# The last phase of a two-layer graph network moved into the second layer's block: sums by GpSimd and TensorE, rows normalised by ScalarE, stored chunk by chunk

## The chip, the core and the metric

One Trainium2 chip, one core. The metric is the device time of the kernel in microseconds, the median of three runs. All times inside the kernel are counted from the start of the span of one profiled execution.

## The reference

Two message-passing layers over a graph of 3125 nodes (160 features: 64 scalars and 32 vectors of 3) and 100,000 edges; each is added to its input and followed by a layer norm. The second one is what matters here:

```python
agg = segment_sum(tp, src, num_segments=N) / DENOM      # tp: one message for each edge
out_s = agg_s @ W_out_s + skip_s                        # 96 wide
out_v = einsum('nmi,mk->nki', agg_v, W_out_v) + skip_v  # 32 vectors of 3
fs = silu(out_s[:, :64])
gv = sigmoid(out_s[:, 64:96])[:, :, None] * out_v
x = layernorm(x + concatenate([fs, gv.reshape(N, -1)]))
```

`silu(a)` is `a * sigmoid(a)`, so one sigmoid of 96 columns gives both gates.

## The kernel before

Nodes are padded to 3200 rows, that is 25 tiles of 128 (`NT`), taken in 5 chunks (`NC`) of 5 tiles (`FT`). Edges are taken in 392 pairs of tiles (`NPAIR`). The first layer runs from 0 to about 1100 us, a node phase follows (`nodes`), and from about 1260 us the second layer (`second_layer`) goes through the pairs: messages are projected by TensorE, summed over equal sources, and added into one of four tables in device memory by GpSimd's indirect DMAs (`scatter`, L681). A table row has 192 columns (`OW`): 96 scalars and 3 x 32 vector columns. Pair `u` with even `u` goes into tables 0 and 1, with odd `u` into tables 2 and 3, so the last four of these DMAs go into tables 0, 1, 2, 3 in this order. After the last, GpSimd waits for all four tables (L688), and the block ends: every engine meets the others there.

The last phase is a block of its own (`c5`, L1257 to L1354):

- SyncE issues ten loads of tables 0 and 1, ScalarE ten of tables 2 and 3 (480 KB each, chunk by chunk, L1275 and L1293). `tabs` has room for all five chunks.
- `sums(m)` on VectorE adds tables 0 and 1 of chunk `m` (L1315), GpSimd adds tables 2 and 3 (L1286), VectorE adds the two halves into `so` (L1318).
- ScalarE takes the sigmoid of 96 columns for each of the chunk's 5 tiles (L1297).
- `update(m - 1)` on VectorE multiplies (L1324, L1325), adds to `xres` (L1330), and takes mean and variance of the 5 tiles (L1333, L1336).
- When all chunks are through, ScalarE takes the roots of all 25 variances (L1299), VectorE refines them (L1362 to L1366) and normalises tile by tile, two instructions for each (L1348, L1350), which also puts the vector columns into the order of the output. SyncE stores a chunk when its five tiles are done (L1278).

On each engine instructions run in the order in which they are written, and DMAs are issued from the engine's own order too.

Of the kernel before, what the change touches and what calls it, by code (L numbers as in the profile page):

```python
# [29 lines left out]
FT = 5  # L30
P = 128
# [31 lines left out]
NPAIR = TILES // 2  # L63
EPS = 1e-5
# [16 lines left out]
def steps(eng, total, body, first, unroll):  # L81

    first = min(-(-first // unroll) * unroll, total)
    last = max(first, total // unroll * unroll)
    for s in range(first):
        body(s, s // unroll, s % unroll)
    if last > first:
        with eng.Fori(first // unroll, last // unroll) as j:
            for r in range(unroll):  # L90
                body(j * unroll + r, j, r)
    for s in range(last, total):
        body(s, s // unroll, s % unroll)

# [11 lines left out]
def gnn_kernel(nc, t, out):  # L106
    top = ExitStack()
    with top:
# [286 lines left out]
        with ExitStack() as cs:  # L395
# [101 lines left out]
            goht_done, gx_ready, gstep, gfeat_done = (sem(cs, n) for n in ("goht_done", "gx_ready", "gstep", "gfeat_done"))  # L497
            joined = sem(cs, "joined")
            block = cs.enter_context(nc.Block())

# [114 lines left out]

            @block.gpsimd
            def _(pool):
# [69 lines left out]
                for tab in range(NTAB):  # L687
                    pool.wait_ge(tab_in[tab], 16 * (TILES // NTAB))  # L688

            @block.scalar  # L690
            def _(act):
# [102 lines left out]
                split_steps(act, NPAIR, 2, step, 4, short=2)  # L794

# [12 lines left out]
            def _(pe):  # L808
# [446 lines left out]
        c4.close()  # L1255

        with ExitStack() as c5:  # L1257
            tabs = sb(c5, "tabs", [P, NC, NTAB, FT, OW])
            tsum = sb(c5, "tsum", [P, 2, 2, FT, OW])
            so = sb(c5, "so", [P, 2, FT, OW])  # L1260
            sg = sb(c5, "sg", [P, 2, FT, 96])
            upd = sb(c5, "upd", [P, 2, FT, D])
            bst5 = sb(c5, "bst5", [P, NT, 6])
            orow = sb(c5, "orow", [P, NC, FT, D])
            tin = [sem(c5, f"tin{i}") for i in range(NC)]
            half_done, half2_done, so_done, sg_done, upd_done, res_done, bs5, mv5 = (
                sem(c5, n) for n in ("half_done", "half2_done", "so_done", "sg_done", "upd_done", "res_done", "bs5", "mv5"))
            lv5, lr5, on_done, ch5, o_out = sem(c5, "lv5"), sem(c5, "lr5"), sem(c5, "on_done"), sem(c5, "ch5"), sem(c5, "o_out")
            block = c5.enter_context(nc.Block())

            @block.sync
            def _(sp):
                for m in range(NC):
                    for k in range(2):
                        sp.dma_start(tabs[:, m, k, :, :], tile_rows(t["tabs"][k], m)).then_inc(tin[m], 16)  # L1275
                for m in range(NC):
                    sp.wait_ge(on_done, m + 1)
                    sp.dma_start(tile_rows(out, m), orow[:, m, :, :]).then_inc(o_out, 16)  # L1278
                sp.wait_ge(o_out, 16 * NC)

            @block.gpsimd
            def _(pool):
                for m in range(NC):
                    pool.wait_ge(tin[m], 16 * NTAB)
                    since(pool, so_done, m - 1)
                    pool.tensor_tensor(tsum[:, m % 2, 1, :, :], tabs[:, m, 2, :, :], tabs[:, m, 3, :, :],  # L1286
                                       ALU.add).then_inc(half2_done, 1)

            @block.scalar
            def _(act):  # L1290
                for m in range(NC):
                    for k in range(2, NTAB):
                        act.dma_start(tabs[:, m, k, :, :], tile_rows(t["tabs"][k], m)).then_inc(tin[m], 16)  # L1293
                for m in range(NC):
                    act.wait_ge(so_done, m + 1)
                    since(act, upd_done, m - 1)
                    act.activation(sg[:, m % 2, :, :], so[:, m % 2, :, 0:96], ACT.Sigmoid).then_inc(sg_done, 1)  # L1297
                act.wait_ge(lv5, 1)
                act.activation(ntmp[:, 0, :], ntmp[:, 1, :], ACT.Sqrt).then_inc(lr5, 1)  # L1299

            @block.vector
            def _(dve):
                done = [0]

                def link(ins):

                    done[0] += 1
                    ins.then_inc(ch5, 1)
                    dve.wait_ge(ch5, done[0])

                def sums(m):

                    r = m % 2
                    dve.wait_ge(tin[m], 16 * NTAB)
                    dve.tensor_tensor(tsum[:, r, 0, :, :], tabs[:, m, 0, :, :], tabs[:, m, 1, :, :], ALU.add).then_inc(half_done, 1)  # L1315
                    dve.wait_ge(half_done, m + 1)
                    dve.wait_ge(half2_done, m + 1)
                    dve.tensor_tensor(so[:, r, :, :], tsum[:, r, 0, :, :], tsum[:, r, 1, :, :], ALU.add).then_inc(so_done, 1)  # L1318

                def update(m):  # L1320

                    r = m % 2
                    dve.wait_ge(sg_done, m + 1)
                    dve.tensor_tensor(upd[:, r, :, 0:S], so[:, r, :, 0:S], sg[:, r, :, 0:S], ALU.mult)  # L1324
                    dve.tensor_tensor(upd[:, r, :, S:D].rearrange("p a (c u) -> p a c u", c=3),  # L1325
                                      so[:, r, :, 96:OW].rearrange("p a (c u) -> p a c u", c=3),
                                      sg[:, r, :, S:96].unsqueeze(2).to_broadcast([P, FT, 3, V]), ALU.mult).then_inc(upd_done, 1)
                    dve.wait_ge(upd_done, m + 1)
                    here = xres[:, m * FT:(m + 1) * FT, :]
                    dve.tensor_tensor(here, here, upd[:, r, :, :], ALU.add).then_inc(res_done, 1)  # L1330
                    dve.wait_ge(res_done, m + 1)
                    for u in range(m * FT, (m + 1) * FT):
                        dve.bn_stats(bst5[:, u, :], xres[:, u, :]).then_inc(bs5, 1)  # L1333
                    for u in range(m * FT, (m + 1) * FT):
                        dve.wait_ge(bs5, u + 1)
                        dve.bn_aggr(mv[:, u, :], bst5[:, u, :]).then_inc(mv5, 1)  # L1336

                for m in range(NC + 1):
                    if m < NC:
                        sums(m)  # L1340
                    if m:
                        update(m - 1)
                dve.wait_ge(mv5, NT)
                layer_norm_scale(dve, link, mv, ntmp, rstd, lv5, lr5, slice(0, NT), 1)
                for u in range(NT):
                    m, at = divmod(u, FT)
                    mean, scale = mv[:, u, 0:1], rstd[:, u:u + 1]
                    dve.tensor_scalar(orow[:, m, at, 0:S], xres[:, u, 0:S], mean, scale, ALU.subtract, ALU.mult)  # L1348

                    last = dve.tensor_scalar(orow[:, m, at, S:D].rearrange("p (u c) -> p c u", c=3),  # L1350
                                             xres[:, u, S:D].rearrange("p (c u) -> p c u", c=3), mean, scale,
                                             ALU.subtract, ALU.mult)
                    if at == FT - 1:
                        last.then_inc(on_done, 1)  # L1354
# [83 lines left out]
```

## Time and profile before

| | |
|---|---|
| median of 3 runs | 2825.72 us (2823.81 to 2827.75) |
| profiled execution | 2825.36 us, its span 2823.5 us, 1.86 us around it |
| last indirect DMA issued by GpSimd | 2748.66 us |
| first load of a table issued | 2755.02 us |
| last VectorE instruction ends | 2820.34 us |
| TensorE's mean granted clock | 0.92 of full speed |

The profiled execution is 0.36 us below the median of the three runs, so differences inside its span can be set against the median.

### The profile page before, as it was taken

To read this page: it belongs to the slowest core of one execution; us is meant where nothing else is said; L and a number is where in the kernel's file an instruction comes from. 1 tells how busy PE (TensorE), PEld (TensorE's weight loads), DVE (VectorE), ACT (ScalarE), POOL (GpSimd) and SP (SyncE) were. 2 spreads that over 40 slices of the span, in tenths; PEclk is the share of its full clock that TensorE was granted. 3 is DMA by queue.
4 is the path that set the end of the run, shared out by engine and by line. 5 is a ranking of instruction groups with operands and counts; after the bars stand their busy time and mean duration, and the time that the engine had idled before them with its cause. 6 is when DMAs were issued, how large, how long until landed. Compare 5 with 4: busy or idle time off the path is not lost. (4 is left out here: it accounts for less than half of the span.)

```text
span 2823.5 us, 80757 instructions
## 1 busy us (share of the span) xinstructions
PE 2604.4 (92%) x24172; PEld 2231.0 (79%) x24172; DVE 1632.9 (58%) x4318; ACT 887.5 (31%) x1988; POOL 2071.6 (73%) x1825
## 2 busy tenths in 40 slices
PE   4799999999999998979999999999999999999970
PEld 2477777777777777868999999999999999999960
DVE  5365555555555555515666666666666666666646
ACT  1111111111111112124444444444444444444430
POOL 3477777777777775236888888888888888888881
PEclk9999899898889888559999999999999999999985
DMA  4333333333333333247888878888888888878765
GB/s 129 106 110 102 107 100 105 101 106 101 101 103 106 102 101 81 99 159 134 143 143 143 142 143 143 143 143 143 143 143 144 143 144 141 145 142 144 141 98 168
DMA packets 388993, 355.58 MB, mean 126 GB/s; under 512 B 60992, under 2 KB 340928, under 8 KB 388416
## 3 DMA queue, kind: packets, MB, share of 16 engines
q0 software_dynamic: 150528, 141.40, 33.4%
q1 hardware_dynamic: 228256, 204.77, 25.7%
q10 hardware_dynamic: 10176, 9.03, 1.1%
q8 instruction: 14, 0.23, 0.0%
q14 instruction: 19, 0.16, 0.0%
HBM read 244.75 MB, written 135.90 MB: 135 GB/s over the span
## 5 line engine op out<-in xcount | busy, mean ns | idle before, releaser
L681 POOL DMA_INDIRECT tab<-summed,sidx x784 | 1218.0, 1554 | 272.2 <-issue 208.9
L634 POOL DMA_INDIRECT gat<-f,gidx x784 | 764.8, 976 | 247.8 <-issue 228.6
L1147 DVE TENSOR_TENSOR prod<-ps_w,xg 128x768 f32<-128x768 f32 x392 | 375.3, 958 | 281.5 <-issue 169.7
L937 PE MATMUL ps_o<-ro_v,prod 128*128 128x96 f32 x3136 | 478.2, 275 | 0.0
L937 PEld LDWEIGHTS ps_o<-ro_v,prod 128*128 128x128 f32 x3136 | 413.2, 192 | 0.0
L927 PE MATMUL ps_w<-hid,wf 64*128 64x128 f32 x4704 | 368.7, 289 | 1.2 <-DVE prod L1147 1.2
L773 ACT ACTIVATE xg<-ps_x 128x768 f32<-128x768 f32 x392 | 296.3, 808 | 199.5 <-PE ps_x L959 193.9
L927 PEld LDWEIGHTS ps_w<-hid,wf 64*128 64x128 f32 x4704 | 293.5, 187 | 69.4 <-issue 44.6
L946 PE MATMUL ps_d<-msg,same 128*128 128x193 f32 x1568 | 332.4, 334 | 1.3 <-ACT summed L792 1.3
L935 PE MATMUL ps_o<-ro_s,prod 96*128 96x96 f32 x1568 | 329.9, 292 | 0.6 <-DVE msg L1158 0.6
L1016 DVE TENSOR_TENSOR ta<-ps_w,gat 128x512 f32<-128x512 f32 x196 | 135.5, 691 | 295.4 <-DMA gat<-f,gidx 237.4
L801 PEld LDWEIGHTS ps_g<-sel,ta 128*128 128x128 f32 x1568 | 208.4, 207 | 116.3 <-issue 59.6
L801 PE MATMUL ps_g<-sel,ta 128*128 128x96 f32 x1568 | 242.2, 302 | 42.3 <-DVE acc_c L1028 40.7
L935 PEld LDWEIGHTS ps_o<-ro_s,prod 96*128 96x128 f32 x1568 | 235.5, 189 | 48.3 <-issue 0.9
L786 ACT ACTIVATE msg<-ps_o 128x192 f32<-128x192 f32 x392 | 130.3, 332 | 445.8 <-PE ps_o L937 444.0
L702 ACT ACTIVATE h<-ps_h 128x256 f32<-128x256 f32 x196 | 75.3, 384 | 593.8 <-PE ps_h L820 583.9
L1154 DVE TENSOR_TENSOR ash<-ps_o,sh 128x192 f32<-128x192 f32 x392 | 140.1, 357 | 191.6 <-ACT msg L786 183.2
L946 PEld LDWEIGHTS ps_d<-msg,same 128*128 128x128 f32 x1568 | 247.9, 192 | 1.6 <-DVE msg L1158 1.6
L792 ACT ACTIVATE summed<-ps_d 128x386 f32<-128x386 f32 x392 | 193.1, 493 | 162.8 <-PE ps_d L946 156.8
L827 PE MATMUL ps_w<-w,h 64*128 64x192 f32 x1568 | 205.2, 384 | 0.0
L827 PEld LDWEIGHTS ps_w<-w,h 64*128 64x128 f32 x1568 | 141.6, 209 | 75.6 <-issue 75.5
L801 PE MATMUL ps_g<-sel,tc 128*96 128x72 f32 x1568 | 193.3, 272 | 0.0
(183 smaller groups left out, 3354.8 us busy)
## 6 DMA issues: line engine op xcount, KB each, us to landing
src_bc<-in_src_rows SPq DMA_DIRECT2D x196, 256.0 KB
tabw<-feat SPq DMA_DIRECT2D x784, 36.0 KB
ea<-in_ea SPq DMA_DIRECT2D x196, 128.0 KB
feat<-fst SPq DMA_DIRECT2D x25, 576.0 KB, 2.8
gat<-f,gidx POOLq DMA_INDIRECT x784
hot_dst<-in_dst_rows SPq DMA_DIRECT2D x98, 128.0 KB
hot_dir<-sh_rows SPq DMA_DIRECT2D x98, 128.0 KB
dst_bc<-hot_dst SPq DMA_DIRECT2D x196, 64.0 KB
```

Of the source, the lines that this page charges most:

```text
L634: pool.indirect_dma_start(out=gat[:, r % 4, k, :], out_offset=None, in_=t["f0"], in_offset=bass.IndirectOffsetOnAxis(ap=gidx[:, r // 4, at ...
L681: pool.indirect_dma_start(out=t["tabs"][into[k]], out_offset=bass.IndirectOffsetOnAxis(ap=sidx[:, r, k:k + 1], axis=0), in_=summed[:, r, k ...
L773: act.activation(xg[:, r, 2 * i:2 * i + 2, :], ps_x4[:, 2 * i:2 * i + 2, 0:3 * P], ACT.Copy)
L792: act.activation(summed[:, ur, :, :], ps_d[:, :, 0:LW], ACT.Copy).then_inc(sum_done, 1)
L801: last = pe.matmul(ps_g[r][0:hi, (n * 4 + lo) * WIN:(n * 4 + up) * WIN], lhs[:, r, k, :, :].rearrange("p a b -> p (a b)"), sel[:, r, k, lo ...
L827: last = pe.matmul(ps_w[r][:, k, 0:192], h2[h:h + S, r, P * (k % 2):P * (k % 2) + P], w3[h:h + S, :], start=True, stop=True)
L927: last = pe.matmul(ps_w4[:, h, P * c:P * c + P], wf2[rows_h, c, :], hid[rows_h, r // 2, at], start=True, stop=True)
L935: pe.matmul(ps_o[:, k, 0:96], prod[0:96, ur % 2, k, 0, :], ro_s[0:96, :], start=True, stop=True)
L937: last = pe.matmul(ps_o[:, k, 96 + 64 * c:192 + 64 * c], prod[:, ur % 2, k, 1 + c, :], ro_v[:, c, :], start=True, stop=True)
L946: last = pe.matmul(ps_d[:, k, 0:LW], same[:, ur // 2, ur % 2 * 2 + k, :], msg[:, ur % 2, k, :], start=True, stop=True)
L1147: dve.tensor_tensor(prod[:, r % 2, :, :, :].rearrange("p k c e -> p k (c e)"), ps_w4[:, :, 0:3 * P], xg[:, r // 2, r % 2 * 2:r % 2 * 2 + 2 ...
L1154: dve.tensor_tensor(ash[:, :, :, :], ps_o[:, :, 96:128].unsqueeze(2).to_broadcast([P, 2, 3, V]), sh[:, bass.ds(u * 2, 2), :].unsqueeze(3). ...
```

## The change

The block `c5` is gone. Its work is appended, on each engine, to the instructions of the second layer in the block before it.

- **Loads.** `load_tables` runs on SyncE for tables 0 and 1 and on ScalarE for 2 and 3. Ahead of the first load of table `k` it waits for that table's scatters alone. `tabs` has room for four chunks (`RING5`), so the fifth chunk's loads wait for the sum of chunk 0 (`so_ready`, `pair_done`).
- **Sums.** GpSimd adds tables 0 and 1 (`pair`). TensorE adds table 2, table 3 and that sum by multiplying each with the identity and accumulating in PSUM: 3 matmuls of 480 columns for each of two halves, f32. Ahead of it, after the last edge pair, TensorE does 10 matmuls of 512 columns whose result nobody reads (`idle_matmuls`).
- **Gate and update.** ScalarE's sigmoid and VectorE's products read the sum from PSUM. The residual is added in two parts, the second of which already writes the output's order of columns, into `orow`, which takes the place of `f1`.
- **Roots.** Each chunk by itself: GpSimd raises the five variances to the power -0.5 (`root5`), VectorE refines in four instructions and makes `-mean * scale` (`scale5`).
- **Normalising.** ScalarE, one activation for each tile: `Identity(scale * x + shift)`, both operands a column (`normalise`). SyncE stores the chunk after its five.

The orders on the engines, for chunks 0 to 4 (g is the gate, n normalise, u update, s scale, p pair, r root):

```
ScalarE  g0 g1 n0 g2 n1 g3 n2 g4 n3 n4
VectorE  u0 u1 s0 u2 s1 u3 s2 u4 s3 s4
GpSimd   p0 p1 r0 p2 r1 p3 r2 p4 r3 r4
```

```diff
+def idle_matmuls(pe, bank, square, count, times=4):
+    for _ in range(count):
+        pe.matmul(bank, square, square.unsqueeze(1).to_broadcast([P, times, P]), start=True, stop=True)
...
+            def load_tables(eng, tables, landed):
+                for m in range(NC):
+                    since(eng, so_ready, m + 1 - RING5)
+                    since(eng, pair_done, m + 1 - RING5)
+                    for k in tables:
+                        if m == 0:
+                            eng.wait_ge(tab_in[k], 16 * (TILES // NTAB))
+                        eng.dma_start(tabs[:, m % RING5, k, :, :], tile_rows(t["tabs"][k], m)).then_inc(landed[m], 16)
...
+                load_tables(sp, (0, 1), tin_a)
+                for m in range(NC):
+                    sp.wait_ge(on_done, FT * (m + 1))
+                    sp.dma_start(tile_rows(out, m), orow[:, m * FT:(m + 1) * FT, :]).then_inc(o_out, 16)
...
-                for tab in range(NTAB):
-                    pool.wait_ge(tab_in[tab], 16 * (TILES // NTAB))
+                def pair(m):
+                    pool.wait_ge(tin_a[m], 32)
+                    since(pool, so_ready, m - 1)
+                    pool.tensor_tensor(tsum[:, m % 2, :, :], tabs[:, m % RING5, 0, :, :], tabs[:, m % RING5, 1, :, :],
+                                       ALU.add).then_inc(pair_done, 1)
+                def root5(m):
+                    tiles = slice(m * FT, (m + 1) * FT)
+                    pool.wait_ge(lv5, m + 1)
+                    pool.tensor_tensor(ntmp[:, 0, tiles], ntmp[:, 1, tiles], a2_col[:, tiles], ALU.pow).then_inc(lr5, 1)
...
+                for m in range(NC + 1):
+                    if m < NC:
+                        pair(m)
+                    if m:
+                        root5(m - 1)
...
+                def gate(m):
+                    act.wait_ge(so_ready, m + 1)
+                    since(act, upd_done, m - 1)
+                    act.activation(sg[:, m % 2, :, :], ps_so[m % 2][:, 0, :, :], ACT.Sigmoid).then_inc(sg_done, 1)
+                def normalise(m):
+                    act.wait_ge(shift_done, m + 1)
+                    for u in range(m * FT, (m + 1) * FT):
+                        act.activation(orow[:, u, :], orow[:, u, :], ACT.Identity, scale=rstd[:, u:u + 1],
+                                       bias=shift[:, u:u + 1]).then_inc(on_done, 1)
+                load_tables(act, (2, 3), tin_b)
+                for m in range(NC + 1):
+                    if m < NC:
+                        gate(m)
+                    if m:
+                        normalise(m - 1)
...
+                pe.wait_ge(relu_done, NGRP)
+                idle_matmuls(pe, ps_x4[:, 0, :], ident[:, :], 10)
+                for m in range(NC):
+                    pe.wait_ge(tin_b[m], 32)
+                    since(pe, sg_done, m - 1)
+                    since(pe, upd_done, m - 1)
+                    pe.wait_ge(pair_done, m + 1)
+                    for h in range(2):
+                        for n, part in enumerate((tabs[:, m % RING5, 2, :, :], tabs[:, m % RING5, 3, :, :], tsum[:, m % 2, :, :])):
+                            last = pe.matmul(ps_so[m % 2][:, h, :, :], ident[:, :], part[:, :, 96 * h:96 * h + 96],
+                                             start=n == 0, stop=n == 2)
+                    last.then_inc(so_ready, 1)
...
+                    dve.tensor_tensor(orow[:, chunk, 0:S], xres[:, chunk, 0:S], upd[:, r, :, 0:S], ALU.add)
+                    dve.tensor_tensor(orow[:, chunk, S:D].rearrange("p a (u c) -> p a c u", c=3),
+                                      xres[:, chunk, S:D].rearrange("p a (c u) -> p a c u", c=3),
+                                      upd[:, r, :, S:D].rearrange("p a (c u) -> p a c u", c=3), ALU.add).then_inc(res_done, 1)
...
+                def scale5(m):
+                    dve.wait_ge(lr5, m + 1)
+                    link5(dve.tensor_tensor(tmp, first, first, ALU.mult))
+                    link5(dve.tensor_tensor(tmp, tmp, var, ALU.mult))
+                    link5(dve.tensor_scalar(tmp, tmp, -0.5, 1.5, ALU.mult, ALU.add))
+                    link5(dve.tensor_tensor(scale, first, tmp, ALU.mult))
+                    dve.scalar_tensor_tensor(tmp, mv[:, chunk, 0], -1.0, scale, ALU.mult, ALU.mult).then_inc(shift_done, 1)
+                for m in range(NC + 1):
+                    if m < NC:
+                        update5(m)
+                    if m:
+                        scale5(m - 1)
```

## Rows read from the trace of the kernel before

**Rows 1.** The chain that ended last, in time: start us, us, what.
```profile
2773.79 2.91 ACTq L1293
2776.72 1.28 ACT L1297
2778.65 0.64 DVE upd L1324
...
2820.03 0.31 DVE orow L1350
```

**Rows 2.** Timeline, end of the scatters: start us, us, engine, line, idle before.
```profile
2744.97 1.54 POOL L681 DMA_INDIRECT tab<-summed,sidx  x1 [0.30 <-DMA tab<-summed,sidx]
...
2748.66 1.54 POOL L681 DMA_INDIRECT tab<-summed,sidx  x1 [0.31 <-issue]
2755.02 20.17 SPq L1275 DMA_DIRECT2D tabs<-tab  x10
```

**Rows 3.** Busy time in stretches of 1 us; the last columns: clock, DMA share, GB/s.
```profile
2751.00:2752.00 1.00, 0.00 (x0) 0.00 (x0) 0.00 (x0) 0.00 (x0) 0.00 (x0) 0.50 0.62 83
2752.00:2753.00 1.00, 0.00 (x0) 0.00 (x0) 0.00 (x0) 0.00 (x0) 0.00 (x0) 0.50 0.00 0
...
2756.00:2757.00 1.00, 0.00 (x0) 0.00 (x0) 0.00 (x0) 0.00 (x0) 0.00 (x0) 0.50 0.66 93
...
2787.00:2788.00 1.00, 0.00 (x0) 0.00 (x0) 0.96 (x3) 0.25 (x1) 0.01 (x1) 0.50 0.09 27
```

**Rows 4.** Groups of instructions from 2762 us on: busy us, mean ns, idle before.
```profile
L1315 DVE TENSOR_TENSOR tsum<-tabs 128x960 f32<-128x960 f32 x5 | 6.1, 1224 | 27.1 <-DMA tabs<-tab 27.1
L1330 DVE TENSOR_TENSOR xres<-xres,upd 128x800 f32<-128x800 f32 x5 | 5.0, 991 | 0.2
L1325 DVE TENSOR_TENSOR upd<-so,sg 128x480 f32<-128x480 f32 x5 | 3.2, 648 | 0.0
L1297 ACT ACTIVATE sg<-so 128x480 f32<-128x480 f32 x5 | 2.9, 599 | 18.5 <-DVE so L1318 18.4
L1324 DVE TENSOR_TENSOR upd<-so,sg 128x320 f32<-128x320 f32 x5 | 2.5, 509 | 3.5 <-ACT sg L1297 3.5
```

**Rows 5.** Timeline: GpSimd's add alone, then GpSimd and VectorE together.
```profile
2776.74 2.21 POOL L1286 TENSOR_TENSOR tsum<-tabs 128x960 f32<-128x960 f32 x1 [2.85 <-DMA tabs<-tab]
...
2787.62 0.99 DVE L1330 TENSOR_TENSOR xres<-xres,upd 128x800 f32<-128x800 f32 x1
2787.99 2.69 POOL L1286 TENSOR_TENSOR tsum<-tabs 128x960 f32<-128x960 f32 x1 [2.39 <-DMA tabs<-tab]
2788.65 1.23 DVE L1333 BATCH_NORM_STATS2 bst<-xres 128x6 f32<-128x160 f32 x5
...
2790.14 1.56 DVE L1315 TENSOR_TENSOR tsum<-tabs 128x960 f32<-128x960 f32 x1
```

**Rows 6.** Groups elsewhere in the kernel, shapes kept apart.
```profile
L285 ACT ACTIVATE frow<-ps_n,a_col 128x160 f32<-128x160 f32 x25 | 9.8, 393 | 49.8 <-PE ps_n L261 49.8
L728 ACT ACTIVATE f<-ps_y 128x160 f32<-128x160 f32 x25 | 7.6, 305 | 44.4 <-PE ps_y L889 44.4
L665 POOL TENSOR_SCALAR fst<-f 128x32 f32<-128x32 f32 x75 | 22.2, 296 | 0.0
L1364 DVE TENSOR_TENSOR ntmp<-ntmp 128x5 f32<-128x5 f32 x5 | 0.9, 171 | 0.2
```

**Rows 7.** Timeline: TensorE's last matmuls of 193 columns.
```profile
2732.27 0.85 PE L946 MATMUL ps_d<-msg,same 128*128 128x193 f32 x4
```

**Rows 8.** Busy time in stretches (PE first), the third column from the end: granted clock.
```profile
1116.00:1120.00 4.00, 4.00 (x21) 4.00 (x21) 2.04 (x9) 3.89 (x6) 0.00 (x0) 0.50 0.60 205
...
1276.00:1280.00 4.00, 2.99 (x32) 2.77 (x36) 2.82 (x5) 0.47 (x2) 0.00 (x0) 0.97 0.55 142
...
2735.00:2737.00 2.00, 0.33 (x3) 0.04 (x1) 0.00 (x0) 0.00 (x0) 1.70 (x2) 1.00 0.50 56
2737.00:2740.00 3.00, 0.00 (x0) 0.00 (x0) 0.38 (x2) 0.49 (x1) 2.39 (x3) 0.53 0.50 46
```

More of the change, by code:

```diff
@@ L63 @@
 NPAIR = TILES // 2
+RING5 = 4
 EPS = 1e-5
@@ L686, in _ @@
                 steps(pool, NPAIR, scatter, 4, 4)
-                for tab in range(NTAB):
-                    pool.wait_ge(tab_in[tab], 16 * (TILES // NTAB))
+                def pair(m):
[7 more added lines that the diff above has]
+                    pool.tensor_tensor(ntmp[:, 0, tiles], ntmp[:, 1, tiles], a2_col[:, tiles], ALU.pow).then_inc(lr5, 1)
+                pool.memset(a2_col[:, :], -0.5).then_inc(half_set, 1)
+                pool.wait_ge(half_set, 1)
+                for m in range(NC + 1):
[3 more added lines that the diff above has]
+                        root5(m - 1)
             @block.scalar
@@ L1253, in _ @@
                     second_layer(sweep)
[L1255 to L1307, printed above, removed]
-                    ins.then_inc(ch5, 1)
[L1309 to L1322, printed above, removed]
@@ L1323, in update, with link5, update5 @@
+                done5 = [0]
+                def link5(ins):
+                    done5[0] += 1
+                    ins.then_inc(ch5, 1)
+                    dve.wait_ge(ch5, done5[0])
+                def update5(m):
+                    r, so = m % 2, ps_so[m % 2]
+                    chunk = slice(m * FT, (m + 1) * FT)
                     dve.wait_ge(sg_done, m + 1)
-                    dve.tensor_tensor(upd[:, r, :, 0:S], so[:, r, :, 0:S], sg[:, r, :, 0:S], ALU.mult)
+                    dve.tensor_tensor(upd[:, r, :, 0:S], so[:, 0, :, 0:S], sg[:, r, :, 0:S], ALU.mult)
@@ L1331, in update @@
                     dve.wait_ge(res_done, m + 1)
                     for u in range(m * FT, (m + 1) * FT):
-                        dve.bn_stats(bst5[:, u, :], xres[:, u, :]).then_inc(bs5, 1)
+                        dve.bn_stats(bst5[:, u, :], orow[:, u, :]).then_inc(bs5, 1)
                     for u in range(m * FT, (m + 1) * FT):
@@ L1336, in update @@
                         dve.bn_aggr(mv[:, u, :], bst5[:, u, :]).then_inc(mv5, 1)
+                    dve.wait_ge(mv5, (m + 1) * FT)
+                    dve.tensor_scalar(ntmp[:, 1, chunk], mv[:, chunk, 1], EPS, None, ALU.add).then_inc(lv5, 1)
+                def scale5(m):
+                    chunk = slice(m * FT, (m + 1) * FT)
+                    first, var, scale, tmp = ntmp[:, 0, chunk], ntmp[:, 1, chunk], rstd[:, chunk], shift[:, chunk]
+                    dve.wait_ge(lr5, m + 1)
[4 more added lines that the diff above has]
+                    dve.scalar_tensor_tensor(tmp, mv[:, chunk, 0], -1.0, scale, ALU.mult, ALU.mult).then_inc(shift_done, 1)
                 for m in range(NC + 1):
                     if m < NC:
-                        sums(m)
+                        update5(m)
                     if m:
[L1342 to L1354, printed above, removed]
+                        scale5(m - 1)
+        c4.close()
 def layer_norm_scale(dve, link, mv, ntmp, rstd, var_ready, root_ready, tiles, turn):
```

19 lines of the change are left out of this document (16 added, 3 removed).

## The prediction

> **What bounds the kernel now.** I read the chain that ended last first, since only what lies on it can be gained. Before the last phase the change alters nothing, so the question is what happens between the last scatter and the end. GpSimd issues the last scatter at 2748.66 [rows 2] and its data moves until about 2752.0 [rows 3]; the first loads are issued at 2755.02 [rows 2]. In the chain ScalarE's own loads come next: its tenth is issued from 2773.79 to 2776.7, since the queue takes no more than it can hold, and only then can ScalarE load its table (1.28 us) and do the first gate, which ends at 2778.63 [rows 1]. From 2778.65 to 2820.34 VectorE is the chain [rows 1]: 41.7 us, ending with the 50 normalising instructions. The store needs the remaining 3.16 us to the end of the span at 2823.5. The loads are no bound in that stretch: their data moves from about 2756.3 to 2787.1 [rows 3], 9.83 MB in 30.8 us, 320 GB/s, and VectorE is behind them.
>
> So the change can gain by an earlier first gate, and by a shorter way from there to the last store.
>
> **The first gate.** ScalarE waits for tables 2 and 3 only and not for the blocks to meet: its first load goes out at about 2750.4 and the second at 2752.3, 2.7 us ahead of 2755.02. SyncE's tables 0 and 1 are complete two DMAs earlier, 3.7 us [rows 2], so its loads run alone from about 2748 to 2752. ScalarE's ten stay its limit. Its tenth was issued when the flow had 10.4 us to go [rows 1, 3], that is 3.5 of its transfers at 2 x 0.49 MB / 320 GB/s = 3.07 us each. Now 6.5 of them must have moved since about 2751.5 (1.3 us from an issue to the first data, as 2755.0 to 2756.3 [rows 2, 3]): 6.5 x 3.07 = 20.0 gives 2771.5. I take 2771.0, as SyncE's lead and its fifth chunk's wait leave ScalarE's queue a bit more of the rate. Table load and gate [rows 1, 4]: 1.28 + 0.60 gives **2772.9**, 5.7 us earlier than 2778.63. Had the lead no effect at all, it would be 2775.
>
> **Costs for each chunk.**
>
> Update on VectorE: 0.40 and 0.65 for the two products (L1324's 509 ns less 0.1 that lies under the next one, and L1325's 648 [rows 4]); the addition of 320 elements 0.43 and of 480, with columns reordered, 0.65 + 0.15 + 0.03, where there was one of 0.99 [rows 4]; statistics 1.5 from their start to that of the next addition [rows 5], with 0.1 as that now has to wait for their end; one more small instruction 0.18 [rows 6]. Sum **4.1**. The 0.15 for reordering is an estimate between 0 and 0.4.
>
> Scale on VectorE: five small dependent instructions of 0.17 with 0.03 between [rows 6], **1.0**.
>
> Normalise on ScalarE: an activation of 160 elements took 305 ns without, 393 with one column operand [rows 6]; with two I estimate 480. They overlap by 0.1, so five take 5 x 0.38 + 0.1 = **2.0**.
>
> GpSimd's pair: 2.2 alone [rows 5]. Its power of 5 elements has no row. Bounds: nothing, and the 2.2 us of its widest add; I take 0.3, as the row nearest in size, 32 elements in 296 ns [rows 6]. This is the least certain price.
>
> TensorE's sum: two matmuls of 193 columns, two records each, last 0.85 us together [rows 7]; less some 0.15 of start-up, an estimate, that is 0.9 ns for a column and record. Six matmuls of 480 columns: 6 x 2 x 480 x 0.9 = **5.2 us** at the full clock, 10.3 at half. The ten idle matmuls (512 columns, 9.2 us) are over at about 2744.5. The clock was at 1.00 up to 2737 and at 0.53 over 2737 to 2740, when TensorE had stopped at 2735.3 [rows 8]. So I expect them to hold 2.4 GHz until some 2 to 4 us behind their end, and chunk 0's sum, which waits for table 3's data until about 2759, to start at 1.2 GHz. They cost nothing, being behind TensorE's last work, and bring nothing.
>
> **A lock between GpSimd and VectorE.** VectorE's add at 2790.14 took 1.56, against a mean of 1.22 with itself included [rows 4]: it ended 1.02 after GpSimd's add, which ended at 2790.68. And that one took 2.69 instead of 2.21 alone; it ended 2.07 after VectorE's addition, which ended at 2788.61 and overlapped it. The statistics in between took the same 1.23 [rows 5]. So two such adds exclude each other. The Trainium skill ("SBUF — State Buffer", section "SBUF: two separate sides") says the same of VectorE's instructions with two SBUF inputs against GpSimd's reads, an exclusive lock for the whole instruction. That VectorE's products, which read one input from PSUM now, are spared by it, no row shows; were they not, pair 2 would stall VectorE by 1 us more.
>
> **The new order makes waits.** p2 on GpSimd is written behind r0, which needs u0's variance; p3 behind r1, p4 behind r2. So each of these pairs starts just when VectorE has finished an update: p2 falls into u1 (its additions wait, 1.5 us), p3 into s0 and p4 into s1, whose small adds of two SBUF inputs wait 2.2 us each. On ScalarE g2 is behind n0, which needs s0, and u2 needs g2: between s and the next u VectorE stands idle for n + g, 2.0 + 0.6 + 0.05, three times (before u2, u3, u4).
>
> **The sum from the first gate's end.** 2772.9; five updates 20.5; p2's stall 1.5; five scales, less the overlaps of their ends, 4.6; power 4 x 0.3 = 1.2; p3 and p4 in the scales 4.4; n + g three times 8.0; at the end n3 and n4 behind the last scale 3.1. That gives 2816.2, where VectorE ended at 2820.3: the way from the first gate has become 43.3 us instead of 41.7, so 1.6 of the 5.7 us won are given back. The store takes 3.16 as before: **2819.4** for the span, 4.1 us less. VectorE's normalising and its ten adds of tables (1.2 us each by L1315 [rows 4]) are gone, but the waits for ScalarE and GpSimd stand in their place. TensorE hides: p2 ends at 2779.6, sum 2 by 2784.8 at the full clock, and g2 cannot start before 2787.9. With 1.86 us around the span and the 0.36 by which the profiled run lies under the median, the forecast is **2821.6**, 0.15% less.
>
> **Rivals.**
>
> *The clock stays at half.* The five sums then take 10.3 us each and are a chain: 2759 to 2769, 2779.6 (sum 1), then from p2 on 2790, 2800.2, 2810.5; g4 ends at 2811.2, u4, s4, n4 and the store follow: span 2823.8, time **2826.0**, no change. For it: at 1116 TensorE was busy the whole 4 us at 0.50 [rows 8], with weight loads all that time. Against: the clock rose at about 1276 [rows 8]. By the Trainium skill ("TensorE: Matmul & The Clock Gate", section "The HAM clock gate (the "warmup" mystery)") sustained matmuls release it, and the sums would not bind; that gives the forecast of 2821.6. Chance 0.2, the forecast 0.42.
>
> *The adds hardly collide.* If GpSimd's adds find no VectorE instruction in their way and the reverse (or the pairs get ahead), p2, p3 and p4 cost nothing: the span is 2813.4 at the full clock, 2816.0 if a sum takes 7.7 us; time 2815.6 to 2818.2, **2816.5**. Chance 0.22. Against it are rows 5.
>
> *The power is dear.* It lies ahead of s and, by r1 and r2, ahead of p3 and p4; 1 us more costs 4 to 5 us in all, once at each chunk. From 1.2 us on the kernel is slower than before; at 2.2, the upper bound, the span is 2827.0, time **2829**; from 2.6 us on, or at 2.2 with the clock at half, it is slower by over 0.2%. Nothing but the missing row speaks for it. Chance 0.12.
>
> *Table swaps.* Identity has no row; Copy and Relu needed no table of their own. If it did, gates and normalising would each load one: seven more of 1.28 us, six of them on the chain, 2829. 
>
> **Range and chances.** From the case without collisions, 2815.5, to the dear power, 2829; the forecast's own range is 2819 to 2824 (reordering 0 to 0.4 five times, first gate up to 2 us later). About 0.2% (5.6 us) is what a measurement can tell. Faster by more: the second rival and a third of the forecast's case, 0.37. Within: the rest of it, the half clock, the table swaps, a part of the dear power, 0.53. Slower: the rest of the dear power, beyond its bound or with the half clock, 0.10.
>
> **What would show it.** First loads at about 2747 (SyncE) and 2750.4 (ScalarE); the first gate ends near 2773; three idle stretches of 2.7 us on VectorE ahead of u2, u3, u4, ended by ScalarE's gate and not by TensorE; the pow's mean near 0.3 us; scales 0 and 1 with one instruction of over 2 us; TensorE's sum 5 to 8 us. If the gates wait for TensorE, the clock was it; if the chain shows GpSimd ahead of the scales, the power. I am wrong if ScalarE's loads no longer hold back the first gate, or if the last phase starts earlier than the scatters let me think.

## The result, and the profile after

The changed kernel takes **2809.31 us** (median of 7 runs, 2805.9 to 2815.2) where the kernel before, beside it, takes 2827.33 (7 runs, 2823.81 to 2832.56): ratio **0.9944**, 95% interval 0.9931 to 0.9958. Forecast were 2821.6 us and a range of 2815.5 to 2829. It is faster by more than the forecast allowed, and the first question is where.

The profiled execution took 2810.92 us, its span 2809.1. The end of the scatters and the new loads, from the timeline (start, duration, engine, line, operation; idle time before it in brackets):

```profile
2738.11 25.98 SPq L529 DMA_DIRECT2D tabs<-tab  x10
...
2740.11 1.55 POOL L717 DMA_INDIRECT tab<-summed,sidx  x1 [0.30 <-issue]
...
2744.24 19.97 ACTq L529 DMA_DIRECT2D tabs<-tab  x10
...
2764.24 1.28 ACT L852 ACT_TABLE_LOAD   x1 [34.73 <-issue]
...
2765.53 0.57 ACT L852 ACTIVATE sg<-ps_x 128x480 f32<-128x480 f32 x1
```

The last scatter, L717, is issued at 2740.11; before it was 2748.66 [rows 2]. So **8.55 of the 14.4 us by which the span shrank are won before the last phase begins**. From that issue to the end of the span it is 68.98 us, where it was 74.88: the last phase, all that the prediction had priced, gave 5.9 us (forecast 4.1).

Where do the 8.55 come from? The instructions of the first layer and of the scatters are the same in both programs. The groups of the page for GpSimd's indirect DMAs (busy us, mean ns of one; idle time before them), first of before:

```profile
L681 POOL DMA_INDIRECT tab<-summed,sidx x784 | 1218.0, 1554 | 272.2 <-issue 208.9
L634 POOL DMA_INDIRECT gat<-f,gidx x784 | 764.8, 976 | 247.8 <-issue 228.6
```

and of after:

```profile
L717 POOL DMA_INDIRECT tab<-summed,sidx x784 | 1217.9, 1553 | 275.0 <-issue 206.9
L670 POOL DMA_INDIRECT gat<-f,gidx x784 | 753.7, 961 | 247.9 <-issue 229.7
```

The scatters cost the same, and from the first to the last of them it is 1460.7 us in both programs. The 784 gathers of the first layer cost 15 ns less each in the mean, 11.1 us together, with the same idle time around them. The view of that line alone shows that it is no handful of long ones (duration ns shortest/middle/longest, first and last start), before and after:

```profile
L634 POOL DMA_INDIRECT gat<-f,gidx x784: 949/954/1341, 93.4 to 1100.6; - x196
```

```profile
L670 POOL DMA_INDIRECT gat<-f,gidx x784: 942/947/1327, 93.3 to 1089.5; - x196
```

The shortest and the middle one are both 7 ns shorter. 764.8 us of gathers and 243 us between them fill the 1007.2 us from the first to the last: GpSimd waits for others in under 20 us of them, so it is the limit of the first layer here, and what one gather saves is passed on. From the last gather to the first scatter the changed kernel took 2.5 us more in this pair of traces (189.9 against 187.4), which is why 11.0 us won by the last gather are 8.55 at the last scatter.

The last phase. First VectorE, GpSimd and ScalarE around updates 1 and 2 and scale 0 in the timeline of after:

```profile
2770.33 1.21 POOL L733 TENSOR_TENSOR ntmp<-ntmp,a_col 128x5 f32<-128x5 f32 x1 [18.85 <-DVE ntmp L1368]
...
2771.52 2.28 POOL L727 TENSOR_TENSOR tsum<-tabs 128x960 f32<-128x960 f32 x1
2771.65 2.81 DVE L1358 TENSOR_TENSOR f<-xres,upd 128x480 f32<-128x480 f32 x1
...
2776.35 1.18 POOL L733 TENSOR_TENSOR ntmp<-ntmp,a_col 128x5 f32<-128x5 f32 x1 [2.56 <-DVE ntmp L1368]
2776.38 0.20 DVE L1376 TENSOR_TENSOR shift<-shift,ntmp 128x5 f32<-128x5 f32 x1
...
2777.01 0.17 DVE L1379 SCALAR_TENSOR_TENSOR shift<-mv,rstd 128x5 f32<-128x5 f32 x1
2777.21 2.17 ACT L857 ACTIVATE f<-f,shift,rstd 128x160 f32<-128x160 f32 x5 [8.65 <-DVE shift L1379]
...
2777.51 2.23 POOL L727 TENSOR_TENSOR tsum<-tabs 128x960 f32<-128x960 f32 x1
...
2780.68 0.57 ACT L852 ACTIVATE sg<-ps_x 128x480 f32<-128x480 f32 x1 [1.30 <-PE ps_x L1077]
...
2781.28 0.49 DVE L1352 TENSOR_TENSOR upd<-ps_x,sg 128x320 f32<-128x320 f32 x1 [4.11 <-ACT sg L852]
```

Pair 2 (L727 at 2771.52) holds VectorE's second addition of update 1 up: 2.81 us, of which 0.80 are its own. The power (L733) takes 1.18 us, not 0.3. But scale 0 runs beside the power, and pair 3, queued behind it, begins at 2777.51, when the scale is over (its last instruction at 2777.01 takes 0.17). Gate 2 then waits 1.30 us for TensorE's sum. The waits of the last phase (us in total, times, longest):

```profile
DVE upd L1352 <- ACT sg L852: 45.7, 4, 36.2
...
ACT f L857 <- DVE shift L1379: 23.9, 4, 8.7
...
PE ps_x L1077 <- POOL tsum L727: 6.0, 1, 6.0
...
ACT sg L852 <- PE ps_x L1077: 3.2, 2, 1.9
DVE shift L1375 <- POOL ntmp L733: 0.4, 1, 0.4
```

The 36.2 in the first line is the wait before update 0, the other three are 4.11, 2.69 and 2.69 ahead of updates 2, 3 and 4. GpSimd's power is waited for once, at the last chunk, for 0.4 us.

TensorE's clock in stretches of after (us; busy us of PE, PEld, DVE, ACT, POOL; granted clock, DMA share, GB/s):

```profile
2745.00:2750.00 5.00, 0.00 (x0) 0.00 (x0) 0.00 (x0) 0.00 (x0) 2.93 (x2) 0.50 1.11 328
2755.00:2760.00 5.00, 4.06 (x5) 1.85 (x6) 0.00 (x0) 0.00 (x0) 0.00 (x0) 0.50 1.11 327
2760.00:2765.00 5.00, 5.00 (x14) 2.35 (x13) 0.00 (x0) 0.76 (x1) 0.00 (x0) 0.98 1.10 327
2770.00:2775.00 5.00, 1.06 (x2) 0.62 (x3) 4.90 (x9) 0.00 (x0) 3.47 (x2) 0.54 0.38 114
2775.00:2780.00 5.00, 5.00 (x11) 2.22 (x10) 2.00 (x15) 2.17 (x5) 3.38 (x2) 0.78 0.00 0
```

The sum of chunk 0 starts at 1.2 GHz at 2755.94, as forecast, and takes 7.2 us; that of chunk 2, after a pause of TensorE from 2768 to 2773.9, starts at 1.2 GHz again and takes 6.7 us, where those of chunks 1, 3 and 4 take 5.0 to 5.1.

### The profile page after: what moved, and what is told of

Read it like the earlier page. It is cut to its first block, busy times and chain, and to the rows that moved or that the text cites. A ratio compares the mean times of both kernels' runs of the same rounds, so it can differ in the third digit from the quotient of the medians.

```text
span 2809.1 us, 80907 instructions
## 1 busy us (share of the span) xinstructions
PE 2640.4 (94%) x24252; PEld 2245.4 (80%) x24252; DVE 1614.1 (57%) x4287; ACT 896.6 (32%) x2011; POOL 2063.3 (73%) x1831
## 4 chain that ended last, share of the span: by engine, by line
PE 65%; POOL 14%; issue 10%; DMA 4%; DVE 2%; SPq 1%; DVEq 1%; ACT 1%; POOLq 0%; ACTq 0%
POOL gat L670 14%; PE ps_o L1008 12%; PE ps_w L998 12%; PE ps_d L1017 9%; PE ps_o L1006 9%; PE ps_x L1030 6%; PE ps_g L872 5%; PE ps_x L983 3%; DMA gat<-f,gidx 2%; PE ps_w L898 2%; PE ps_h L886 1%; PE ps_h L891 1%; PE ps_r L942 1%; DMA tab<-summed,sidx 1%; PE ps_y L959 1%
## 5 line engine op out<-in xcount | busy, mean ns | idle before, releaser
L717 POOL DMA_INDIRECT tab<-summed,sidx x784 | 1217.9, 1553 | 275.0 <-issue 206.9
L670 POOL DMA_INDIRECT gat<-f,gidx x784 | 753.7, 961 | 247.9 <-issue 229.7
```

The source lines that it names most:

```text
L670: pool.indirect_dma_start(out=gat[:, r % 4, k, :], out_offset=None, in_=t["f0"], in_offset=bass.IndirectOffsetOnAxis(ap=gidx[:, r // 4, at ...
L717: pool.indirect_dma_start(out=t["tabs"][into[k]], out_offset=bass.IndirectOffsetOnAxis(ap=sidx[:, r, k:k + 1], axis=0), in_=summed[:, r, k ...
```

## The experiments

Twelve runs of eleven versions. "Last phase" is the time from the issue of the last scatter to the end of the span.

**Both kernels once more, side by side, and the new tiles alone.** The third is the kernel before with the change's tiles declared and unused:

```diff
+            tabs = sb(c4, "d_tabs", [P, RING5, NTAB, FT, OW])
+            tsum = sb(c4, "d_tsum", [P, 2, FT, OW])
+            sg = sb(c4, "d_sg", [P, 2, FT, 96])
...
+            shift = sb(c4, "d_shift", [P, NT])
```

> The kernel before, unchanged, traced once more. In the trace after the change the first layer's gathers, a stretch 1500 us ahead of the edit, took 11.0 us less than before: 784 of them, from the first issue to the last 1007.2 us before and 996.2 after, their median 954 and 947 ns, the gaps between them the same 305 ns. Theory A (the program as a whole, its layout or its length, sets this price): here again a median of 954 and a stretch of about 1007 us. Rival B (it varies from execution to execution): a median anywhere between 945 and 956 and a stretch between 995 and 1010 us, without regard to the kernel. The last phase, from the last scatter's issue to the end of the span, 74.8 us within 0.5 by both.

> The kernel after, unchanged, traced once more. Theory A: gathers with a median of 947 ns and a stretch of about 996 us. Rival B: anything between 995 and 1010 us. The last phase 69.0 us within 1 by both; what can move in it is where the clock rises and falls.

> The kernel before, which also declares the new tiles of the last phase beside the second layer's tiles and uses none of them. Nothing else is changed, so the instructions are the same. Theory A1 (where tiles lie sets the gathers' price): the first layer's stretch near 996 us. Rival A2 (the programs' instructions set it) and rival B: 1007 us, or what the kernel before shows beside it. The last phase 74.8 us by all.

Measured: 2828.06, 2820.22 and 2833.27 us. Last phases 74.80, 70.11 and 74.89. Gathers, shortest/middle: 950/957, 942/949, 950/957 ns. The view of the third:

```profile
L642 POOL DMA_INDIRECT gat<-f,gidx x784: 950/957/1341, 93.4 to 1103.7; - x196
```

So the cheap gathers come again with the change, and declaring these tiles is not the cause. Single runs differ by some microseconds in the first layer anyway: the gathers' waits for VectorE are 16.3, 16.7 and 20.5 us here, with no order by kernel. The shortest and middle duration is the steady sign.

The last phase of the changed kernel, 70.11 us, is just outside what was expected (69.0 within 1). Three parts are longer than in the first trace: the first gate ends 26.3 us after the last scatter's issue instead of 26.0, the wait ahead of update 2 is 4.24 instead of 4.11, and ahead of update 4 VectorE waits 3.39 instead of 2.69, because the sum of chunk 4 starts at 1.2 GHz here (granted clock 0.50 from 2797.6 to 2801.0) and is on the path too.

**No idle matmuls.**

```diff
-                idle_matmuls(pe, ps_x4[:, 0, :], ident[:, :], 10)
```

> The kernel after without the ten idle matmuls. My theory from before the result: they bring nothing, since the clock is at half again before chunk 0's sum, so the last phase is 69.0 us within 0.5. Rival C (they hold the clock or shift its periods so that the sums of chunks 0 to 2 are shorter): 70 to 73 us, with the second or third gate later than now. For the first layer: Theory A2 (the programs' instructions set the gathers' price): within 1 us of the kernel after if only TensorE's program matters little.

Measured: 2806.99 us; last phase 70.34, against 70.11 with them. By its figure alone 70.34 lies in the rival's range of 70 to 73 and not within 0.5 of 69.0, but the kernel with the matmuls, traced beside it, is as long. So they are worth nothing there, as forecast. The 13 us by which this run is under the changed kernel beside it lie upstream (last scatter at 2734.82 instead of 2748.28), where the programs are the same; with one run of each this says nothing on the matmuls.

**The last phase in a block of its own again**, with the changed kernel's work in it. One thing isn't as before: GpSimd's wait for all four tables ahead of the end of the second layer's block is not there.

```diff
+            blocks.close()
+            block = cs.enter_context(nc.Block())
...
+            @block.sync
+            def _(sp):
+                load_tables(sp, (0, 1), tin_a)
```

> The kernel after with its new last phase in a block of its own, as it was before: the engines meet behind the last scatters, and only then are loads issued. Same instructions otherwise. Last phase (last scatter's issue to the end of the span): the early loads are worth the 4.0 us by which the first gate ended sooner, so 73.0 us within 1; rival (the wait of the blocks is hidden, the gain is all in the new order of work): 69 us. First layer: if the number of blocks sets the gathers' price, their median is 954 to 957 ns and the shortest 949; if the instructions of the last phase do, 946 to 949 and 942.

Measured: 2809.98 us; last phase 72.10, with its last scatter issued at 2735.41 and its loads here:

```profile
2739.87 20.00 SPq L1287 DMA_DIRECT2D tabs<-tab  x10
...
2739.89 21.66 ACTq L1287 DMA_DIRECT2D tabs<-tab  x10
```

They go out 4.5 us after that scatter, where in the kernel before it was 6.4 [rows 2]. The first gate ends 28.0 us after it; before 30.0, in the changed kernel 26.0 or 26.3. So loads ahead of the block's end are worth 72.10 less 70.11 or 68.98, 2.0 to 3.1 us, and the 2.8 us by which this version is shorter than the kernel before are for the greater part (1.9) the earlier meeting of the engines. From the first gate on it takes 44.1 us, before 44.9. The gathers are the cheap ones (942/946), so it isn't the structure of blocks that makes them so.

**No power on GpSimd.** The roots become additions of the same size, so the scales are other numbers:

```diff
-                    pool.tensor_tensor(ntmp[:, 0, tiles], ntmp[:, 1, tiles], a2_col[:, tiles], ALU.pow).then_inc(lr5, 1)
+                    pool.tensor_tensor(ntmp[:, 0, tiles], ntmp[:, 1, tiles], a2_col[:, tiles], ALU.add).then_inc(lr5, 1)
```

> The kernel after with the power replaced by an addition, so that the scales are wrong. In the trace after the power took 1.18 us and the whole chain of a scale (1.0 us) ran beside it, so that pairs 3 and 4 began only when the scale was over. Theory D (the dear power is what kept the pairs off the scales): with an operation of some 0.2 us pairs 3 and 4 start 0.9 us earlier and fall into scales 0 and 1, one of whose instructions lasts over 2 us, and the last phase is 1 to 3 us longer than 69. Rival E (small adds of 5 elements do not collide with a pair): scales as now, the last phase 68 to 69 us. For the first layer: if the power makes the program load other code on GpSimd, the gathers' median goes back to 954; if not, 947.

Measured: 2814.76 us; last phase 71.49, **longer** than with the dear power (68.98 and 70.11). GpSimd, then VectorE, in the timeline:

```profile
2772.53 2.21 POOL L727 TENSOR_TENSOR tsum<-tabs 128x960 f32<-128x960 f32 x1
...
2777.70 0.20 POOL L733 TENSOR_TENSOR ntmp<-ntmp,a_col 128x5 f32<-128x5 f32 x1 [2.96 <-DVE ntmp L1368]
2777.86 2.21 POOL L727 TENSOR_TENSOR tsum<-tabs 128x960 f32<-128x960 f32 x1
```

```profile
2772.61 0.64 DVE L1353 TENSOR_TENSOR upd<-ps_x,sg 128x480 f32<-128x480 f32 x1
2773.29 1.80 DVE L1357 TENSOR_TENSOR f<-xres,upd 128x320 f32<-128x320 f32 x1
...
2777.72 0.20 DVE L1376 TENSOR_TENSOR shift<-shift,ntmp 128x5 f32<-128x5 f32 x1
2777.95 2.14 DVE L1377 TENSOR_SCALAR shift<-shift 128x5 f32<-128x5 f32 x1
...
2787.64 2.13 DVE L1377 TENSOR_SCALAR shift<-shift 128x5 f32<-128x5 f32 x1
```

With the root at 0.20 us, pair 3 starts inside scale 0 and pair 4 inside scale 1, and one instruction of each scale takes over 2 us: the two collisions of the prediction. They add 3.9 us; the stall in update 1 is 1.3 us instead of 2.0, and the wait for sum 2 is gone, so from the first gate on it takes 44.8 us instead of 43.0. In the changed kernel the power of 1.18 us is what keeps the pairs off the scales. The first two lines of VectorE also settle what the prediction left open: the product, which reads one input from PSUM, ran beside pair 2 and kept its 0.64 us, and the addition behind it, with both inputs in SBUF, had to wait. And the gathers are the dear ones again:

```profile
L670 POOL DMA_INDIRECT gat<-f,gidx x784: 949/953/1337, 93.5 to 1091.9; - x196
```

This is the changed program with one operation swapped in code that runs some 1680 us after the last gather. In time the single run does not show what the power is worth: its last scatter is issued at 2741.44, 1.3 us later than in the first trace of the changed kernel and 6.8 us earlier than in the second. GpSimd waited for VectorE for only 7.0 us in its first layer, against 13.7 and 16.7 in those two.

**A power alone, in the kernel before**, at the start of its last phase; its result is read by nobody. And its control, with `ALU.add` in the same place:

```diff
+                pool.memset(pw[:, :, :], 1.0).then_inc(pw_set, 1)
+                pool.wait_ge(pw_set, 1)
+                pool.tensor_tensor(pw[:, 0, :], pw[:, 0, :], pw[:, 1, :], ALU.pow).then_inc(pw_done, 1)
```

> The kernel before, to which GpSimd gets one power of 128x5 elements at the start of its last phase, where it waits for the tables anyway; nobody reads the result. In the traces so far the shortest of the 784 gathers of the first layer is 942 ns in all six kernels with a power, and 949 or 950 in the four without, among them the kernel after with the power replaced by an addition. Theory P (a power anywhere in the program changes what each gather costs GpSimd, although it runs 1500 us later): shortest 942, median 946 to 949, the stretch of gathers 5 to 11 us shorter than 1007 to 1010, and a time 0.2 to 0.5% below the kernel before beside it; the last phase 74.8 us. Rival Q (something else in the new last phase does it): shortest 949 or 950, median 953 to 957, no change of time.

Measured: 2814.14 us (11 runs) against 2822.3 (17 runs): ratio **0.9969**, 95% interval 0.9958 to 0.998, that is 8.7 us (5.6 to 11.9). Last phase 74.96, unchanged. (The last phase is from the profiled execution, the longest of the 11.) The added instruction and the gathers:

```profile
2749.13 1.21 POOL L1287 TENSOR_TENSOR pw<-pw 128x5 f32<-128x5 f32 x1
```

```profile
L634 POOL DMA_INDIRECT gat<-f,gidx x784: 942/946/1332, 93.6 to 1090.6; - x196
```

> The control for the power: the kernel before, with a GpSimd tensor_tensor of 128x5 that adds instead of one that raises to a power, in the same place at the start of the last phase, its result read by nobody. If it is the power itself that makes the first layer's gathers cheaper, nothing changes against the kernel before: shortest gather 949 or 950 ns, middle one 953 to 957, ratio within 0.2% of 1. If it is any further instruction, tile or semaphore on GpSimd (where its instructions lie in memory, say), the gathers take 942 and 946 ns as with the power, and the ratio is near 0.997.

> The kernel before with one GpSimd power of 128x5 at the start of its last phase, result unused, once more, beside the same kernel with an addition. If the power makes the gathers cheaper, it shows again: shortest gather 942 ns, middle one 946, ratio 0.996 to 0.998 against the kernel before. If the first time was the chip or chance, the gathers are those of the addition and the ratio is that of the addition.

These two ran together on a chip on which every kernel, the one before too, was granted a mean clock of 0.82 to 0.83 instead of 0.91 to 0.93. Measured: 3272.08 us with the addition and 3271.71 with the power, against 3269.02 before; ratios 1.0005 (0.998 to 1.003) and 1.0009 (0.9978 to 1.004). For the addition, gathers and ratio are those expected if it is the power itself. For the power the gathers are as expected and the ratio is not (0.996 to 0.998). With the addition, then with the power, and what GpSimd waited for ahead of them (us, times):

```profile
L634 POOL DMA_INDIRECT gat<-f,gidx x784: 947/953/1327, 93.5 to 1514.6; - x196
its engine sat idle before it (us, times) until:
  DVE tc L1020: 423.7, 103
```

```profile
L634 POOL DMA_INDIRECT gat<-f,gidx x784: 940/946/1332, 93.5 to 1523.5; - x196
its engine sat idle before it (us, times) until:
  DVE tc L1020: 445.8, 122
```

The power again takes 7 ns from the shortest, the middle and the mean gather (981 to 974), and an addition in its place takes none. But here the gathers stretch over 1421 and 1430 us, not 1007, and GpSimd waits over 400 us of that for VectorE, where it was 15 us at the usual clock; what the gathers save is only waited longer. The likely reason for VectorE's delay is TensorE, which was granted 0.68 from 100 to 1100 us instead of 0.90, but the trace doesn't follow the wait that far. So a gain in time was measured only where GpSimd is the limit. The addition was never timed there: that those 8.7 us belong to the power, and not to the tile, the memset and the instruction that came with it, rests on the gathers' durations.

**All pairs ahead of all roots**, so that GpSimd's additions run while VectorE still waits (`tsum` gets five places):

```diff
-                for m in range(NC + 1):
-                    if m < NC:
-                        pair(m)
-                    if m:
-                        root5(m - 1)
+                for m in range(NC):
+                    pair(m)
+                for m in range(NC):
+                    root5(m)
```

> The kernel after with GpSimd doing all five pairs ahead of the first root (five places for the sums instead of two). No pair falls into update 1 (2.0 us) and the third sum does not hold the third gate (1.3 us): my theory gives 3.3 us less in the last phase, 65.7 us. Rival (the third gate then waits for normalising anyway, and only the collision is saved): 67 us.

Measured: 2805.48 us, ratio 0.9942 (0.9922 to 0.9962); last phase 68.45, a miss by 2.8, and longer than the rival's 67 too. GpSimd shows why:

```profile
2768.82 2.21 POOL L726 TENSOR_TENSOR tsum<-tabs 128x960 f32<-128x960 f32 x1 [8.46 <-DMA tabs<-tab]
2770.99 2.36 POOL L732 TENSOR_TENSOR ntmp<-ntmp,a_col 128x5 f32<-128x5 f32 x2
```

The fifth pair waits for its tables until 2768.82, and the first root stands behind it until 2770.99. Scale 0 begins 2.1 us late by it; the rest of the miss is the first gate, which ends 26.7 us after the last scatter's issue here.

**The same with each gate ahead of the normalising before it.**

```diff
+                gate(0)
                 for m in range(NC + 1):
-                    if m < NC:
-                        gate(m)
+                    if m + 1 < NC:
+                        gate(m + 1)
                     if m:
                         normalise(m - 1)
```

> As the one before, and on ScalarE each gate ahead of the normalising of the chunk two before it (order g0 g1 g2 n0 g3 n1 g4 n2 n3 n4). My theory, that VectorE stands idle for normalise and gate ahead of updates 2, 3 and 4 (2.7 us each), gives another 8 us less: last phase 57.5 to 58.5 us, VectorE without a gap of over 1.5 us between the first product and the last scale. Rival (TensorE's sums, which need the gates and updates two before, become the bound): 60 to 63 us, with gaps ended by TensorE by way of the gates.

Measured: 2798.49 us, ratio **0.9914** (0.9892 to 0.9936); last phase **59.07**, 0.6 over the expected 57.5 to 58.5. Ahead of scale 0 VectorE stands for the root behind the fifth pair, 1.17 us, its only gap of over 0.5 us after the first gate:

```profile
2768.59 0.89 DVE L1367 TENSOR_SCALAR ntmp<-mv 128x5 f32<-128x5 f32 x1
2770.65 0.17 DVE L1374 TENSOR_TENSOR shift<-ntmp 128x5 f32<-128x5 f32 x1 [1.17 <-POOL ntmp L732]
```

**And the first root ahead of the fifth pair** (p0 p1 p2 p3 r0 p4 r1 r2 r3 r4):

```diff
-                for m in range(NC):
+                for m in range(NC - 1):
                     pair(m)
-                for m in range(NC):
+                root5(0)
+                pair(NC - 1)
+                for m in range(1, NC):
                     root5(m)
```

> The kernel of the eighth run with root 0 ahead of pair 4 on GpSimd. There pair 4 had to wait for the fifth chunk's tables until 2767.2, with root 0 and root 1 behind it, and scale 0 began 2.1 us after update 1 ended. With root 0 ahead of it scale 0 follows update 1 at once: the last phase 57 us instead of 59.1 (56.5 to 58), VectorE without a gap between update 1 and scale 0. Rival (update 2 then waits for its gate, and the sums of TensorE take over): 58 to 59.5 us.

Measured: 2796.06 us (6 runs), ratio 0.9911 (0.9892 to 0.993); last phase 58.27, not the expected 56.5 to 58 but in the rival's range, though not for the rival's reason. The gap is gone, but the fifth pair, from 2769.46, now holds a small instruction of VectorE's:

```profile
2770.43 1.27 DVE L1369 TENSOR_SCALAR ntmp<-mv 128x5 f32<-128x5 f32 x1
```

Between the last two the difference is less than their intervals. Both beat the changed kernel, by their ratios to the kernel before, 0.991 against 0.994, by some 9 us, and their last phases are 10 to 12 us shorter than its. Each last phase is from one trace; the interval of 0.9914 still touches the changed kernel's, that of 0.9911 just doesn't.

## Why the prediction was wrong

**The step that failed is its first: "Before the last phase the change alters nothing."** It alters the price of the first layer's gathers, 7 ns for each, through the powers that it puts among GpSimd's instructions (one is enough). Of the 12.3 us between 2821.6 and 2809.3, 8.55 were won ahead of the last phase in the profiled executions; 1.8 in the last phase; the rest, 2.0, is how the profiled executions stand to their medians (0.36 under it before, 1.6 above it after). Shown is: with a power in the program the shortest gather took 940 to 942 ns, in nine traces of seven versions; without one 947 to 950, in five traces of four; swapping the operation alone did it in both directions; and the power alone gave 0.9969 where GpSimd limits the first layer. That is enough for most of what was won ahead of the last phase, but perhaps not for all. By the ratios the changed kernel gained 15.8 us, and its last phase is 4.7 to 5.9 shorter; 10 to 11 remain, where the power alone gave 8.7 (5.6 to 11.9). At the usual clock GpSimd's waits for VectorE among the gathers were 14.8 to 20.5 us in the four traces of the kernel before and its variants, and 6.1 to 16.7 in the eight of the changed kernel and its variants, the one without the power among them. Whether a second, smaller effect of the change lies there stays open.

Not shown is why an operation at the end of a program cheapens DMAs issued over 1650 us ahead of it. Nor do the 7 ns, 5.5 us for 784, account for all of the 8.7: the mean fell by more (975 ns to 959), since the longer ones became fewer or shorter, which stays open too.

The last phase, by the prediction's steps:

- **First gate: mis-sized.** It was to end 24.2 us after the last scatter's issue; it ended 26.0 after it (before 30.0 [rows 1, 2]). ScalarE's first load went out 4.1 us after that scatter, not 1.7: that load waits for table 2, which was complete later than assumed (it goes out 2.8 to 4.1 us after the last scatter's issue in the traces of the versions with early loads). The early loads gave 4.0 us and not 5.7. A slip in the sum made little of this: the 10.4 us that the flow had to go are 3.4 transfers of 3.07 and not 3.5, 0.3 us. The loads of ScalarE are still its limit, as the chain said.
- **Power: mis-sized by four.** 1.18 against 0.3. The size of the operand said nothing: the same instruction as an addition took 0.20. The price was 0.02 us under the point at which the rival of the dear power was to end behind the kernel before, and yet that rival did not come: scales 0 to 3 use a root finished while VectorE was at the next update, and only the last waits for it, 0.4 us instead of four times.
- **Collisions: one of three.** p2 in update 1 cost 2.0 us (1.5 forecast). p3 and p4 in the scales, 4.4 us, did not happen, because the step that put them there rested on the cheap power: at 1.2 us they begin when the scale is over. Two wrong steps met. With the cheap root both were there, 2.14 and 2.13 us, but in a `TENSOR_SCALAR`, which has one SBUF input, and not in one of the additions of two SBUF inputs that the prediction named. The Trainium skill ("SBUF — State Buffer", section "Who interferes with whom") counts single-input instructions in a two-port mode among those that block. The traces agree as far as they go; the mode of an instruction they do not show: `TENSOR_SCALAR` of 5 columns took 2.14, 1.27 and 0.89 us instead of 0.17 beside an addition of GpSimd, while statistics and their aggregation beside one kept their 1.23 and 0.43.
- **Updates, scales, normalising: right.** An update without a stall 4.0 (forecast 4.1), a scale 1.0, five activations 2.17 (2.0), waits for ScalarE of 2.69 ahead of updates 3 and 4, and ahead of update 2 of 4.11, of which 1.3 is TensorE's; no table load between; the idle matmuls bring nothing.
- **TensorE: half right.** About 5 us at the full clock, the first sum starting at half. That a sum would not be on the path failed once: sum 2 takes 6.7 us after TensorE's pause and g2 waits 1.3 us for it. In the second trace it failed at sum 4 as well.
- **The way from the first gate to the end of ScalarE's work: 39.9 instead of 43.3 us.** Minus 4.4 for the two collisions and 0.8 for the power, plus 0.5 in update 1, 1.3 for sum 2 and 0.5 for three longer normalisings; the rest, half a microsecond, is tenths. The store takes 3.1.

So the last phase was 26.0 + 39.9 + 3.1 = 69.0 us, where the prediction had 24.2 + 43.3 + 3.2 = 70.7. That it came within 1.8 us is in part luck: 1.8 too little at the first gate, 4.4 too much for collisions that did not happen and 1.3 missing for sum 2 partly cancel. The order in which the change queues pairs, roots and gates costs some 10 us, which the last two versions get back.

## What to carry to other kernels

Compare the cost of unchanged instructions first when two programs differ: here most of the gain lay in 784 DMA issues that the diff does not touch, each 7 ns cheaper or more, and this counted only where GpSimd was the limit. Where engines take turns, write down their queues: an item that is ready late (the fifth chunk's pair, a normalising) must not stand ahead of one that another engine waits for; here two reorderings without any new instruction shortened a phase of 69 to 70 us by some 10. And a price that serves as a delay elsewhere is not simply added: making the root six times cheaper made this phase 1.4 to 2.5 us longer.

## What the runs showed of the hardware that was not expected

- A program with a tensor_tensor power on GpSimd, tried at two places in the last phase, had indirect gathers 7 ns shorter than the same program with an addition or nothing there (shortest 949 to 942 ns, and at a mean clock of 0.82 947 to 940). The scatters' middle duration is 1542 or 1543 ns without and 1545 or 1546 with it.
- A power of 128x5 takes GpSimd 1.16 to 1.21 us, an addition of that size 0.20. While it ran, VectorE's small instructions of two SBUF inputs kept their 0.16 to 0.20, unlike larger ones beside an addition of 128x960 (0.80 became 2.81).
- A product of VectorE with one input in PSUM and one in SBUF kept its 0.64 us beside GpSimd's addition of 128x960; the addition of two SBUF inputs right behind it took 1.80 instead of 0.49.
- One chip granted TensorE a mean clock of 0.82 in every run of these kernels, the others 0.91 to 0.93: the kernel before took 3269 us there and 2822 on another, and in the first layer GpSimd waited over 400 us for VectorE instead of 15.
